# Values of a cross attention by Strassen's seven block products, two steps behind the scores

## The reference, cut to what matters

```python
q = (inputs_q @ Wq).reshape(b, sq, H, HD) * (1.0 / np.sqrt(HD))   # 128 x 16 x 128
k = (inputs_kv @ Wk).reshape(b, skv, H, HD)                       # 12544 x 16 x 128
v = (inputs_kv @ Wv).reshape(b, skv, H, HD)
scores = jnp.einsum('bqhd,bkhd->bhqk', q, k)
attn = jax.nn.softmax(scores, axis=-1)
ctx = jnp.einsum('bhqk,bkhd->bqhd', attn, v).reshape(b, sq, H * HD)
return ctx @ Wo
```

## Time and profile before

| | |
|---|---|
| median of 3 runs | 2122.44 us (2121.5 to 2127.71) |
| profiled execution | 2124.15 us, span 2122.3 us |
| TensorE busy | 2054.2 us, 97% |
| VectorE busy | 1161.2 us, 55% |
| ScalarE busy | 910.0 us, 43% |
| GpSimd busy | 154.4 us, 7% |
| DMA | 43% of 16 engines, 97 GB/s |

### The profile page before, as it was taken

One profiled execution on the slowest core, in us unless ns is written; L12 is line 12 of the kernel. 1 busy time (PEld: TensorE's weight loads), 2 busy tenths in 40 slices (PEclk: granted clock), 3 DMA queues, 4 the chain that ended last, 5 costly groups with the idle time before them and its releaser, 6 DMA issues.

```text
span 2122.3 us, 30139 instructions
## 1 busy us (share of the span) xinstructions
PE 2054.2 (97%) x11196; PEld 1108.1 (52%) x11200; DVE 1161.2 (55%) x2703; ACT 910.0 (43%) x1985; POOL 154.4 (7%) x209
## 2 busy tenths in 40 slices
PE   5899999999999999999999999999999999999886
PEld 5655555555555555555555555555555555555562
DVE  5664545555555546566666565455555555554426
ACT  3444545444445344344444444444444444443312
POOL 1100101000000101000001001010000010000001
PEclk8999999999999999999999999999999999999998
DMA  5433544444535345464544453343433443532660
GB/s 165 120 69 77 110 88 112 91 102 97 106 84 114 71 94 113 94 129 90 118 104 110 103 112 71 84 90 66 99 72 84 80 86 69 98 63 52 191 218 5
DMA packets 516705, 206.79 MB, mean 97 GB/s; under 512 B 418864, under 2 KB 502832, under 8 KB 515664
## 3 DMA queue, kind: packets, MB, share of 16 engines
q1 hardware_dynamic: 516560, 204.88, 43.4%
HBM read 97.59 MB, written 4.46 MB: 48 GB/s over the span
## 4 chain that ended last, share of the span: by engine, by line
PE 93%; DVE 4%; issue 1%; ACT 1%; DMA 1%; POOL 0%; DVEq 0%; SPq 0%; POOLq 0%; ACTq 0%
PE ps_s L1119 24%; PE ps_t L1119 18%; PE ps_c L1143 12%; PE ps_b L1143 12%; PE ps_a L1143 12%; PE ps_u L1143 12%; PE ps_b L1097 1%; DVE bulk L777 1%; PE ps_t L1201 1%; DMA bulk<-in_vo 1%; PE ps_s L1080 0%; PE ps_c L1108 0%; PE ps_s L1244 0%; PE ps_b L1108 0%; PE ps_u L1268 0%
## 5 line engine op out<-in xcount | busy, mean ns | idle before, releaser
L1119 PE MATMUL ps_s<-bulk 128*128 128x384 f16 (+2 forms) x3264 | 579.0, 321 | 23.3 <-DVE bulk L777 23.2
L1119 PE MATMUL ps_t<-bulk 128*128 128x384 f16 (+2 forms) x2448 | 450.0, 320 | 1.5 <-ACT ps_t L630 1.0
L1119 PEld LDWEIGHTS ps_s<-bulk 128*128 128x128 f16 x3264 | 315.6, 99 | 237.0 <-DVE bulk L777 26.2
L1119 PEld LDWEIGHTS ps_t<-bulk 128*128 128x128 f16 x2448 | 235.6, 98 | 151.4 <-ACT ps_t L630 1.9
L630 ACT ACTIVATE ps_t<-ps_s 128x384 f32<-128x384 f32 (+2 forms) x136 | 62.9, 462 | 583.4 <-PE ps_s L1119 583.4
L1143 PE MATMUL ps_u<-nring,pt 128*128 128x512 f16 x1194 | 269.1, 379 | 0.0
L1143 PE MATMUL ps_a<-nring,pt 128*128 128x512 f16 x1194 | 269.1, 379 | 0.0
L500 POOL TENSOR_TENSOR stages<-stages 128x256 f32<-128x256 f32 x196 | 146.0, 745 | 1677.3 <-DMA stages<-in_ctx 1658.8
L1143 PE MATMUL ps_b<-nring,pt 128*128 128x512 f16 x1158 | 260.7, 379 | 0.0
L1143 PE MATMUL ps_c<-nring,pt 128*128 128x512 f16 x1158 | 260.7, 379 | 0.0
L823 DVE SCALAR_TENSOR_TENSOR pp<-prob,pp 128x768 f16<-128x768 f32 (+2 forms) x272 | 239.7, 923 | 0.0
(11 more groups left out here) (200 smaller groups left out, 1677.7 us busy)
## 6 DMA issues: line engine op xcount, KB each, us to landing
stages<-in_ctx SPq DMA_DIRECT2D x392, 128.0 KB, 2.8
wst<-in_w SPq DMA_DIRECT2D x64, 256.0 KB, 3.4
bulk<-in_vo SPq DMA_DIRECT2D x16, 512.0 KB, 4.9
acc<-in_qk SPq DMA_DIRECT2D x12, 512.0 KB, 5.0
pt<-pp SPq DMA_TRANSPOSE x272, 4.0
tern_d<-wter SPq DMA_DIRECT2D x32, 128.0 KB, 3.0
bulk<-tern_d SPq DMA_DIRECT2D x2, 2048.0 KB, 11.6
wst<-in_qk SPq DMA_DIRECT2D x4, 512.0 KB, 5.9
```

What stands on the lines that cost most here:

```text
L1119: ins = mm(out, q_part(e, qlo, a)[:, c * P:(c + 1) * P], t_moving(k, tlo, b, c), start=(first and c == 0 and qlo == 0 and tlo == 0), stop= ...
```

## The change

The values are made by Strassen's seven products as well. The left matrix is the two heads' turned probabilities (rows of blocks: heads; columns: halves of the chunk), the right one the context chunk (rows of blocks: its halves; columns: halves of the 512). So each value pass moves 256 columns instead of 512, and a chunk has 7 x 3 passes instead of 4 x 3. What follows from it:

- GpSimd makes the four sums of probability blocks (`sum_p`, up to 384 columns each, after the exponentials), and `sum_t` now runs for the values' context stages too.
- The high and low parts of the probabilities, and `pp` and `pt`, have seven blocks instead of four; ScalarE and VectorE write them in five instructions each (three plain blocks at once, then four sums one by one). The low parts stand in step k itself, behind `value_sum_d`, not at the start of step k+1.
- The values' output sums go through PSUM: three ScalarE copies of 256 columns (`value_a`, `value_e_u`) and two VectorE sums (`value_sum_d`, `value_sum_e`) a step, and TensorE waits for `va_copied`, `vu_copied`, `ve_copied` and `vd_done` between the seven products.
- The natural context ring `nring` holds seven blocks, split in one instruction of 1792 elements instead of 1024.
- To make room: one context stage instead of two (a load waits for the split before it), three `qk_slot`s instead of four, `un`, `ut`, `ot`, `x2`, constants and `wg1`, `wg2` placed in other tensors, the constants loaded after the loop and `x` a second time. `aw_o` is loaded with `aw_k` and `aw_v`.
- `q_lo_part` and `q_hi_part` are made a step earlier. `quant` runs in every other of 64 steps instead of in 32 in a row, and now stands ahead of the values' sums. `P_SCALE` is halved.
- The values of the last two steps stand together behind `finish(0)`.

The core of the diff:

```diff
             def turn_p(k, g):
-                sp.wait_ge(lo_done[g], k + 1)
+                sp.wait_ge(lo_done, 5 * k + (2, 5)[g])
                 if k >= LAG:
-                    sp.wait_ge(u_done[g], k - 1)
+                    sp.wait_ge(v4_done, k - 1)
...
+            sp.wait_ge(in_pt[1], 16 * NS)
+            sp.dma_start(diff[:, :], diff_d).then_inc(in_const, 16)
...
+            def sum_p(k):
+
+                for n, (dst, a, b, op) in enumerate(((S1, A21, A22, ALU.add), (S3, A11, A21, ALU.subtract),
+                                                     (S2, S1, A11, ALU.subtract), (S4, A12, S2, ALU.subtract))):
+                    if n == 0:
+                        pool.wait_ge(exp_done[0], k + 1)
+                        if k:
+                            pool.wait_ge(lo_done, 5 * k)
...
+                    if n == 1:
+                        pool.wait_ge(exp_done[1], k + 1)
+                    if n >= 2:
+                        pool.wait_ge(p_sum, 4 * k + n - 1 + (n == 3))
+                    nc.gpsimd.tensor_tensor(prob_part(k, dst), prob_part(k, a), prob_part(k, b), op).then_inc(p_sum, 1)
...
+            for k in range(NS):
+                found = prep_at(k)
+                if found is not None:
+                    sum_t(found[0])
+                sum_p(k)
...
+            def value_a(k):
+                act.wait_ge(v1_done, k + 1)
+                if k:
+                    act.wait_ge(acc_done[0], k)
+                nc.scalar.activation(val_b, val_a, ACT.Copy).then_inc(va_copied, 1)
+
+            def value_e_u(k):
+                act.wait_ge(v5_done, k + 1)
+                act.wait_ge(d_done, min(k + 1 + LAG, NS))
+                nc.scalar.activation(part_e[:, 0:BLK], val_e, ACT.Copy).then_inc(ve_copied, 1)
+                act.wait_ge(v6_done, k + 1)
+                if k:
+                    act.wait_ge(ve_done, k)
+                nc.scalar.activation(part_v[:, :], val_b, ACT.Copy).then_inc(vu_copied, 1)
...
                 exp_head(k, 0)
+                if k >= LAG:
+                    value_a(k - LAG)
                 exp_head(k, 1)
-                if k + 1 < NP:
-                    q_hi_part(k + 1)
+                if k >= LAG:
+                    value_e_u(k - LAG)
...
-                for g in range(2):
-                    act.wait_ge(exp_done[g], k + 1)
-                    if k:
-                        act.wait_ge(in_pt[g], 16 * k)
-                    nc.scalar.activation(pp_part(k, g, 0), prob_of(k, g), ACT.Copy, scale=P_SCALE).then_inc(hi_done[g], 1)
+                hi_part(k, A22, 3, 0)
+                hi_part(k, S1, 1, 1)
+                hi_part(k, S3, 1, 2)
+                hi_part(k, S2, 1, 3)
+                hi_part(k, S4, 1, 4)
...
+            def value_sum_d(k):
+                v.wait_ge(v7_done, k + 1)
+                v.wait_ge(ve_copied, k + 1)
...
+                nc.vector.tensor_tensor(val_d, val_b, part_e[:, 0:BLK], ALU.add).then_inc(vd_done, 1)
...
             def step(k):
-                if k:
-                    lo_head(k - 1, 0)
-                    lo_head(k - 1, 1)
                 v.wait_ge(s2_done, k + 1)
                 max_head(k, 0)
...
                 split_lo(k)
...
-                if 0 <= k - QUANT_AT < 2 * WP:
-                    quant(k - QUANT_AT)
+                if 0 <= k - QUANT_AT < 4 * WP and (k - QUANT_AT) % 2 == 0:
+                    quant((k - QUANT_AT) // 2)
+                if k >= LAG:
+                    value_sum_d(k - LAG)
+                lo_part(k, A22, 3, 1)
+                lo_part(k, S1, 1, 2)
+                lo_part(k, S3, 1, 3)
+                lo_part(k, S2, 1, 4)
+                lo_part(k, S4, 1, 5)
...
+                if k >= LAG:
+                    value_sum_e(k - LAG)
+                add_values(k - LAG, 1)
+                add_values(k - LAG, 0)
...
+            def values(k):
...
+                value_product(k, val_a, A11, B11, True, False).then_inc(v1_done, 1)
...
+                value_product(k, val_e, S1, T1, True, False).then_inc(v5_done, 1)
+                pe.wait_ge(in_pt[1], 16 * (k + 1))
+                pe.wait_ge(va_copied, k + 1)
+                value_product(k, val_b, S2, T2, False, False).then_inc(v6_done, 1)
+                value_product(k, val_a, A12, B21, False, True)
+                pe.wait_ge(vu_copied, k + 1)
+                value_product(k, val_b, S3, T3, False, False).then_inc(v7_done, 1)
+                pe.wait_ge(ve_copied, k + 1)
+                value_product(k, val_e, S4, B22, False, True).then_inc(v3_done, 1)
+                pe.wait_ge(vd_done, k + 1)
+                value_product(k, val_b, A22, T4, False, True).then_inc(v4_done, 1)
```

More of the change, by code:

```diff
@@ L34 @@
 Q_SCALE = 16.0
-P_SCALE = 2.0 ** 15
+P_SCALE = 2.0 ** 14
 EXP_SCALE = float(HD) ** -0.5 / (CTX_SCALE * Q_SCALE)
@@ L317, in perceiver_layer @@
         al_done = sem("al_done")
-        hi_done = [sem(f"hi_done{g}") for g in range(2)]
-        lo_done = [sem(f"lo_done{g}") for g in range(2)]
-        u_done = [sem(f"u_done{g}") for g in range(2)]
+        hi_done = sem("hi_done")
+        lo_done = sem("lo_done")
+        p_sum = sem("p_sum")
+        v1_done = sem("v1_done")
+        v5_done = sem("v5_done")
+        v6_done = sem("v6_done")
+        v7_done = sem("v7_done")
+        v3_done = sem("v3_done")
+        v4_done = sem("v4_done")
+        va_copied = sem("va_copied")
+        ve_copied = sem("ve_copied")
+        vu_copied = sem("vu_copied")
+        vd_done = sem("vd_done")
+        ve_done = sem("ve_done")
+        in_xr = sem("in_xr")
         r_done = sem("r_done")
@@ L937, in _ @@
             o_copy(0)
+            value_sum_d(NS - 2)
+            value_sum_e(NS - 2)
+            add_values(NS - 2, 1)
+            add_values(NS - 2, 0)
+            value_sum_d(NS - 1)
+            value_sum_e(NS - 1)
+            add_values(NS - 1, 1)
             add_values(NS - 1, 0)
-            add_values(NS - 1, 1)
             norm_head(2)
@@ L1149, in step, with value_product @@
-            def step(k, between=None):
+            def value_product(k, dst, a, b, first, last):
+                _, lowest, w = STEPS[k]
+                g = a // PURE
+                for n in range(w):
+                    c = next(c for c in range(lowest, lowest + w) if ring_slot(c) == window(k)[4][n])
+                    for plo, clo in ((0, 0), (0, 1), (1, 0)):
+                        tile = pt_at(k) + p_at(k, g, plo, a % PURE) + n * P
+                        ins = mm(dst, pt[:, tile:tile + P], n_part(c, clo, b), start=(first and n == 0 and plo == 0 and clo == 0),
+                                 stop=(last and n == w - 1 and plo == 1), skip_group_check=True)
+                return ins
@@ L1150, in step @@
+            def step(k):
                 _, a, w = STEPS[k]
@@ L1182, in _ @@
                 step(k)
-            for g, n in chunks(NS - 2):
-                values(NS - 2, g, n)
             def turn(f):
@@ L1213, in _ @@
             finish(0)
-            for g, n in chunks(NS - 1):
-                values(NS - 1, g, n)
+            values(NS - 2)
+            values(NS - 1)
             for f in range(1, H):
```

389 lines of the change are left out of this document (199 added, 190 removed).

## The result

The changed kernel takes 2248.01 us (median of 4 runs, 2245.74 to 2249.19) against 2125.07 us for the kernel before in the same comparison (2121.5 to 2128.38, 4 runs): a ratio of 1.0578, 95% interval 1.0554 to 1.0601. It is 5.8% slower. The forecast was 2,214 with a range of 2,065 to 2,275, and slower with 0.71; the sign and the range held, and the time was 34 us longer than the forecast.

What follows compares the result with a forecast made beforehand. TensorE, busy 97% of the span, was taken as the bound. Columns -116, turns +166, quant +19, split steps +10, start-up +5 and tail +8 gave +92 us on 2,122: 2,214, range 2,065 to 2,275.

Steps and rivals of the forecast that it cites:

- the turns: Loop: GpSimd sums and two-SBUF-input VectorE instructions alternate, delaying the seventh score product or a copy; 1.34 us a step, +166 us.
- the smaller terms: Outside columns and turns: quant +19, split steps' sums and exponential +10, start-up +5, tail +8 us.
- start-up: First steps: query's low part made earlier, against a full VectorE and its blocked time; -15 to +15, taken +5 us.
- Columns: Value products: 21 passes of 256 columns replace 12 of 512, 0.297 us less on 392 chunk visits; -116 us, 13.70 a step.
- `quant`: Three instructions in 32 steps, ahead of value_sum_d, may take turns with GpSimd's sums; 0 to +38, taken +19 us.
- split exponential: Split steps: sums ahead of the maximum and the longer exponential; 0 to +19, taken +10 us.
- Tail: After the loop: last two steps' values with small copies, late transposes, constants and weight loads; 0 to +20, taken +8 us.
- (a): Rival, faster: sharing costs less than the 1.15 us slack a step, one turn instead of five; 2,040 us, chance 0.22.
- (b): Rival, between: a 384-column sum takes 0.8 us or context sums precede low parts, halving the wait; 2,095 to 2,155, chance 0.12.
- (c): Rival, heavier: ScalarE, waiting for GpSimd's last sum, delays split_hi; stage steps lose 3 us, 2,320 us, chance 0.08.
- (d): Rival: TensorE's 256-column passes don't keep 109 ns with another weight each; no chance of its own.
- what would make it wrong: Low parts at 0.55 us beside GpSimd, TensorE idle under 0.3 us a step, waits at va_copied or vd_done, or late transposes.

Runs made afterwards that it cites:

- run 1: Changed kernel with GpSimd's four probability sums a step replaced by memsets of the same blocks (values then wrong): 2095.1 us, ratio 0.9851 to the kernel before.
- 3: Changed kernel with the four probability sums a step moved from GpSimd to VectorE, between quant and value_sum_d: 2131.05 us, ratio 1.0024 to the kernel before.
- run 5: Changed kernel with probability sums on VectorE and GpSimd's context sums waiting for the low parts of the step before: 2096.91 us, ratio 0.987.
- Run 4: Changed kernel with one added wait: GpSimd's context sums start after the five low parts of the step before: 2155.35 us, ratio 1.0129 to the kernel before.
- 7: Kernel before plus four idle GpSimd sums of 384 columns a step, released by the step's a copy, all-reduce moved: 2181.33 us, ratio 1.0262.
- run 9: Kernel before plus four idle GpSimd sums a step, released by the second add_values to meet quant and low parts, all-reduce moved: 2222.8 us, ratio 1.045.
- 8: Kernel before plus four idle GpSimd sums a step, released by the second exponential, all-reduce moved: 2133.74 us, ratio 1.003.
- run 6: Changed kernel with the next query and key weights issued ahead of the context chunks in SP's list: 2236.71 us, ratio 1.0521 to the kernel before.
- run 10: Changed kernel: sums on VectorE, context sums delayed, weights first; first value stage in step 0, paired quants and all-reduce in stage-free steps: 2066.01 us, ratio 0.9722.
- run 11: Fastest kernel until then (2066.01 us) with value_a between split exponential parts and, in the first eight steps, an earlier a copy: 2074.28 us, ratio 0.9747.

## Why the prediction was right, and where it was not

The sign and the cause came as forecast. That the loop's sum, 195 us, met the measured 188 so well is luck in part: the turns were taken 35 us too high and the smaller terms 33 too low. The 34 us that the whole is off are start-up.

**Columns: right.** The steps without a stage take 13.70 us, the figure worked out from the 109 ns of the narrow steps. In 124 steps that is -112 us.

**Turns: the mechanism right, the size 35 us too high.** The place (the seventh product, by the line of L801; and the third, by the a copy) and the cause stand: without the sums' reads (run 1), without the sums on GpSimd (3 and 5) or with one wait in another place (4) the loss goes, and turns alone in the kernel before (7 and 9) bring a loss at the seventh product in the steps whose slack the `quant`s use up, while the same work elsewhere (8) costs 0.3%. In the eight steps from 1,811 us on, the loss over 13.70 (13.95 in split steps) is 0.78 where the stages begin (forecast 1.1; the next such step, not split, has 1.03), then four times 1.6 and once 1.09 (forecast five times 1.8), 0.45 in the step behind them (0.6), and 0. Sixteen steps ahead of the quants (from 457 us on) take 238.1 us; less 16 x 13.70 and 8 x 0.25 this is 16.9, or 1.06 a step and 131 us in 124 steps, not 166. A sum of 384 columns alone lasts 1.00 us (median of the idle ones), forecast 1.02, a low part 0.552, forecast 0.55, a step's transposes 6.5, forecast 5.8, and TensorE waits for them 0.6 us in the whole loop.

**Smaller terms in the loop: too low by about as much.** `quant` cost 33 us (forecast 19, bound 38): 64 steps around it take 984.6 us, four times the 238.0 of the 16 plain ones behind them is 952.0. One of the 64 has a granted clock of 0.95, so up to 2 us of this is TensorE's clock. Its instructions do take turns, though they read one SBUF block each:

```profile
L941 DVE TENSOR_SCALAR wter<-wst 128x512 bf16<-128x512 f32 x32 | 35.3, 1103 | 1.1
L935 DVE TENSOR_SCALAR wst<-wst,wsc 128x512 f32<-128x512 f32 x32 | 33.2, 1036 | 0.0
```

They took 0.43 and 0.48 before. My sentence "with one SBUF input it is free" was drawn from a copy out of PSUM and is wrong for these. The split exponential cost 0.25 us in every other step, 15 us (forecast 10), read from the steps without a stage: TensorE waits for `va_copied`. The all-reduce cost 14 us in one step (29.1 us long), and no term stood for it. The change puts it into GpSimd's list among sums that the path now depends on. GpSimd's timeline there, and TensorE's first values behind it:

```profile
717.56 0.41 POOL L591 PARTITION_ALL_REDUCE wsc<-wsc  x1 [5.62 <-issue]
...
725.84 3.12 POOL L561 TENSOR_TENSOR stage<-stage 128x256 f32<-128x256 f32 x4 [7.87 <-issue]
...
732.23 2.08 PE L1227 MATMUL ps_w<-nring,pt 128*128 128x256 f16 x9 [12.14 <-ACT ps_w L672]
```

The instruction counts 0.41 us, but 5.62 ahead of it and 7.87 behind it GpSimd waits for nothing that the profile shows: 13.9 us in all, in which no sum runs. ScalarE waits for those sums with its split, and so TensorE waits 12.14 us for `va_copied`. Behind this wait its next three groups of nine passes start 1.9 us apart instead of 0.98, at 1.2 GHz: some 3 us more of the step. That the 13.9 equal the 14 lost is chance. Before, GpSimd had nothing else to do there. 131 + 33 + 15 + 14 = 193, against 188 measured (15.22 - 13.70 a step, the first of the 124 lose less) and 195 forecast.

**Start-up: the step that failed.** "I take +5", with a bound of +15; it was +39. I had counted L777's shift and left two queues unread. The shift gave more than I hoped: TensorE's wait for the query's low part fell from 23.2 to 2.7 us. In its place stand 18.8 for the a copy, 9.2 for `value_sum_d` and 12.2 for weights (the rows at run 6). The clock adds to it. The same stretch of the kernel before:

```profile
24.98:123.50 98.52, 78.11 (x570) 60.16 (x570) 68.63 (x139) 49.10 (x89) 12.55 (x12) 0.90 0.43 111
```

Between its waits TensorE now ran more of the time at 1.2 GHz, a granted clock of 0.81 where it was 0.90, and was busy 86.4 us instead of 78.1, with fewer columns to move. So of the 36 us that the seven steps lost 28 are waits and 8 busy time.

Of the single causes, the query's weights, with three slots and behind context chunks that wait longer, cost 10.2 us (run 6). The values' first context chunk shares the one context stage and is split ahead of step 0: ScalarE's `split_hi` of it waits for four GpSimd sums ahead of the first a copy; TensorE waits 7.5 us for this copy, and 1.9 in run 10, where the stage is moved. Turns took about 5 (run 5: 157.7 for 162.9). Weights first and the stage moved, together and without turns, bring the eighth step to 144.3. Some 20 us remain over the kernel before; in run 10 TensorE waits 15.5 us for the a copy in three narrow steps (18.8 in five in the changed kernel) and 12.5 for `value_sum_d`. Ahead of the a copy ScalarE's list holds the high parts of the sums and the query's high part; run 11 showed that moving the a copy alone makes it worse. What order would be right there stays open.

**Tail: right.** +10 us, forecast +8.

**Rivals.** (a), that turns fit into the slack, needed one turn instead of five. Run 5 comes closest to that case, by an edit: a gain as its sum says, though 2,097 and not 2,040. Run 4, with fewer turns, is still 1.3% slower than the kernel before. (b) did not come: a sum of 384 columns takes 1.00 us, not 0.8, and the context sums did run beside the low parts. (c) did not come, and (d) fell with the 13.70. Of "what would make it wrong" two things came in part: the waits inside the values, 35 us at `vd_done` (25 of them in the stretch of the quants, the rest at start-up) and 20 at `va_copied` (12 of them in the all-reduce's step), beside the 89 at the seventh product.

## What to carry to other kernels

Before work moves to GpSimd, list what VectorE does in the same stretch: its two-input instructions and its scalar operations from SBUF to SBUF took turns with GpSimd's reads here, and the price was not their sum but what was left of it past the slack of the queue they stand in. One wait that keeps the two apart gave back 93 of 123 us without less work; moving 2.2 us a step to the busier of the two engines gave back 117. And count the prologue as carefully as the loop: in its seven steps and ahead of them a slot fewer, a shared stage and a longer list for ScalarE cost 39 us, more than any of the smaller terms of 124 steps.

## What the runs showed of the hardware that was not expected

- A GpSimd memset of 384 columns lasts 0.42 us both beside a two-input VectorE instruction and alone; a copy or a sum waits for that instruction.
- VectorE's scalar operations from SBUF to SBUF on 512 columns go from 0.43 and 0.48 us to between 1.0 and 1.1 beside GpSimd sums.
- A GpSimd all-reduce over partitions that counts 0.41 us kept the engine from its other work for 13.9 us.
- Where both engines have work queued they alternate, one instruction each: three sums among three VectorE instructions cost 2.4 us, 0.8 each. With 0.15 us of each beside the other this is 1.00 less 0.15 to 0.2, as in the earlier trace rows.
- TensorE's clock can fall in the middle of a loop: in run 9, where TensorE waited 2.0 us in the steps before, six of 32 steps had a granted clock of 0.91 and lasted 1.7 us more than the others. What sets these six apart no run shows.
